# A graph network with a mixture of experts: where VectorE forms the next group's logits, and where the split rows' messages are kept

## The reference, cut to what matters

```python
z = (x @ W).reshape(N, heads, dim)
el = sum(z * attn_l); er = sum(z * attn_r)          # one number per node and head
e = leaky_relu(el[src] + er[dst], 0.2)
alpha = softmax of e over the edges of each dst
out = segment_sum(alpha * z[src], dst) + z + bias
```

## Time and profile before

| | |
|---|---|
| median of 3 runs | 3047.59 us (3047.36 to 3049.39) |
| profiled execution | 3049.01 us |
| its span, first to last instruction | 3047.3 us |
| mean granted TensorE clock | 0.966 |
| TensorE busy in the span | 88% |
| VectorE, ScalarE, GpSimd busy | 67%, 41%, 49% |
| edge sweeps (ends rounded) | 250 to 893, 1097 to 1741, 1940 to 2582 us |

### The profile page before, as it was taken

One profiled execution on the slowest core, in us unless ns is written; L12 is line 12 of the kernel. 1 busy time (PEld: TensorE's weight loads), 2 busy tenths in 40 slices (PEclk: granted clock), 3 DMA queues, 4 the chain that ended last, 5 costly groups with the idle time before them and its releaser, 6 DMA issues.

```text
span 3047.3 us, 57262 instructions
## 1 busy us (share of the span) xinstructions
PE 2681.5 (88%) x14059; PEld 1839.2 (60%) x14060; DVE 2055.3 (67%) x3890; ACT 1244.9 (41%) x2607; POOL 1495.0 (49%) x1528
## 2 busy tenths in 40 slices
PE   3997999998989979999899899788899888659998
PEld 2884555555558855555555588555555555447776
DVE  6776888888887768888878877455555555663332
ACT  1224555555554445555555544222323223521111
POOL 1005666666632156666666411466666664114443
PEclk9998999999999979999999999799999999979999
DMA  6448988989968889999989678888888998967776
GB/s 211 167 146 269 304 306 303 304 306 302 305 203 213 212 247 305 303 307 304 306 299 306 231 199 221 237 295 297 294 300 298 294 297 270 406 211 146 145 146 119
DMA packets 218702, 787.26 MB, mean 258 GB/s; under 512 B 44050, under 2 KB 75938, under 8 KB 217983
## 3 DMA queue, kind: packets, MB, share of 16 engines
q0 software_dynamic: 127632, 604.14, 63.8%
q1 hardware_dynamic: 73230, 133.39, 14.3%
q10 hardware_dynamic: 17760, 48.79, 4.0%
HBM read 665.13 MB, written 133.50 MB: 262 GB/s over the span
## 4 chain that ended last, share of the span: by engine, by line
PE 53%; DVE 22%; issue 13%; ACT 3%; another core or an unknown queue 3%; DMA 2%; SPq 2%; POOL 1%; DVEq 1%; ACTq 1%; POOLq 0%
PE PS L1026 29%; DVE arena L1466 6%; PE PS L957 5%; PE PS L1153 5%; PE PS L1142 4%; PE PS L959 3%; DVE parts L1483 3%; PE PS L1001 2%; DVE W L1466 2%; DMA arena<-table,src_k 2%; SPq L479 1%; DVE arena L1341 1%; DVE arena L1330 1%; DVE arena L1331 1%
## 5 line engine op out<-in xcount | busy, mean ns | idle before, releaser
L652 POOL DMA_INDIRECT arena<-table,src_k x945 | 946.9, 1002 | 488.6 <-issue 225.2
L1026 PE MATMUL PS<-arena,S 128*128 128x384 f32 (+1 forms) x1848 | 694.7, 509 | 58.6 <-issue 49.5
L1466 DVE TENSOR_TENSOR arena<-arena,PS 128x768 f32<-128x768 f32 x630 | 575.0, 945 | 0.9 <-issue 0.5
L1026 PEld LDWEIGHTS PS<-arena,S 128*128 128x128 f32 x1848 | 333.0, 192 | 275.3 <-issue 142.3
L1026 PE MATMUL PS<-parts,S 128*128 128x384 f32 (+2 forms) x1332 | 338.6, 374 | 54.2 <-issue 41.3
L652 POOL DMA_INDIRECT W<-table,src_k x300 | 297.8, 993 | 155.4 <-issue 68.9
L1026 PE MATMUL PS<-arena,S_weighted 128*128 128x384 f32 (+1 forms) x840 | 318.7, 515 | 35.3 <-issue 32.9
L1001 PEld LDWEIGHTS PS<-erp,ST_b 128*128 128x128 bf16 x3735 | 194.8, 97 | 240.6 <-issue 173.1
L598 POOL DMA_DIRECT2D table<-arena x75 | 41.7, 555 | 560.1 <-DVEq L1353 384.2
L809 ACT ACTIVATE apart<-iota_row,dst_k 128x128 f32<-128x128 f32 x830 | 261.5, 389 | 58.4 <-issue 34.4
L1026 PEld LDWEIGHTS PS<-parts,S 128*128 128x128 f32 x1332 | 223.5, 192 | 99.8 <-issue 90.2
(11 more groups left out here) (286 smaller groups left out, 4275.1 us busy)
## 6 DMA issues: line engine op xcount, KB each, us to landing
local_b<-local SPq DMA_DIRECT2D x249, 160.0 KB
mixed<-sums ACTq DMA_DIRECT2D x75, 384.0 KB
arena<-mixed SPq DMA_DIRECT2D x75, 384.0 KB, 4.3
table<-arena POOLq DMA_DIRECT2D x50, 396.0 KB, 3.6
arena<-table SPq DMA_DIRECT2D x50, 384.0 KB, 4.8
arena<-table,src_k POOLq DMA_INDIRECT x945
table<-arena POOLq DMA_DIRECT2D x25, 384.5 KB, 4.8
out<-last_bias POOLq DMA_DIRECT2D x25, 384.0 KB, 6.3
```

Of the source, the lines that this page charges most:

```text
L652: nc.gpsimd.indirect_dma_start(edge_row(l, k % U)[:, 0:table_width(l)], None, table[l][:, :], bass.IndirectOffsetOnAxis(src_k[:, k:k + 1]. ...
L1026: o = nc.tensor.matmul(flat[:, bass.ds(odd * 1024 + 512 * c, n)], onehot, row[:, c * HALF:c * HALF + n], start=False, stop=True, skip_grou ...
L1466: nc.vector.tensor_tensor(z, z, a, ALU.mult).then_inc(s_msg, 1)
```

## The change

- `ER_LEAD` becomes 2, and two groups share a bank: `group_bank(jj)` is bank 4 + jj % 2. TensorE makes the destination terms of group g + 2 in one batch of 15 matmuls, ahead of visit 4 of group g and behind a wait for that group's fifth message.
- Banks 6 and 7 hold one row, `exact_row`. With 12 heads VectorE writes a split row's message there instead of in place, and copies its 12 weights beside it (a new small instruction); ScalarE and the subtraction read it there. The message waits until the split row before it has its rest. Where rows j - 2 and j are both split (10 and 12), the rest of j - 2 stands ahead of message j.
- With one head ScalarE makes the scaled row once more, in fp32, in `exact_row` (a new instruction and a new wait for the rest before), and the rest is a plain subtraction from it.
- VectorE does all steps of the next group's logits, and then `turned`, behind the fifth message of the group.
- With one head the column numbers are copied into two banks rather than four.

```diff
-ER_LEAD = 3
+ER_LEAD = 2
...
         def group_bank(jj):
-            return PS[:, 4 + jj, :]
+            return PS[:, 4 + jj % 2, :]
...
+        def exact_row(n):
+
+            return flat_banks(6)[:, 0:n]
...
                         if H > 1:
-                            nc.scalar.activation(parts[:, n, 0, 0:D + H], row[:, 0:D + H], ACT.Copy).then_inc(s_leading, 1)
+                            nc.scalar.activation(parts[:, n, 0, 0:D + H], exact_row(D + H), ACT.Copy).then_inc(s_leading, 1)
                         else:
                             weight = row[:, D:D + 1]
+                            act.wait_ge(s_rest, len(SPLIT[l]) * i + (n + split_before(l)))
+                            nc.scalar.activation(exact_row(D), row[:, 0:D], ACT.Copy, scale=weight)
...
                         for j in range(G):
+                            if j == G - 1 and ahead:
+                                pe.wait_ge(s_msg, g * G + (V * l + G))
+                                for n in range(G):
+                                    er_of_edges(g + ER_LEAD, (jj + ER_LEAD) % NBUF, n, later[n])
                             add_up(g, i, jj, j, now[j])
                             if j == 0 and ahead:
                                 later = blocks_of(g + ER_LEAD)
-                            if j in (1, 3) and ahead:
-                                for n in ((0, 1), (2, 3, 4))[j // 2]:
-                                    er_of_edges(g + ER_LEAD, (jj + ER_LEAD) % NBUF, n, later[n])
...
-                        nc.vector.tensor_tensor(z, z, a, ALU.mult).then_inc(s_msg, 1)
+                        if at in SPLIT[l]:
+                            held = SPLIT[l].index(at) + split_before(l)
+                            if not isinstance(i, int) or i or held:
+                                dve.wait_ge(s_rest, len(SPLIT[l]) * i + held)
+                            nc.vector.tensor_tensor(exact_row(D).rearrange("p (h d) -> p h d", h=H), z, a, ALU.mult)
+                            nc.vector.tensor_copy(exact_row(D + H)[:, D:D + H], weights_of(l, jj)[:, j, :]).then_inc(s_msg, 1)
+                        else:
+                            nc.vector.tensor_tensor(z, z, a, ALU.mult).then_inc(s_msg, 1)
...
-                        nc.vector.tensor_tensor(low[:, 0:D + H], row[:, 0:D + H], f32(high[:, 0:D + H]), ALU.subtract).then_inc(s_rest, 1)
+                        nc.vector.tensor_tensor(low[:, 0:D + H], exact_row(D + H), f32(high[:, 0:D + H]), ALU.subtract).then_inc(s_rest, 1)
...
-                        nc.vector.scalar_tensor_tensor(out=low[:, 0:D], in0=row[:, 0:D], scalar=weight,
-                                                       in1=f32(high[:, 0:D]), op0=ALU.mult, op1=ALU.subtract).then_inc(s_rest, 1)
+                        nc.vector.tensor_tensor(low[:, 0:D], exact_row(D), f32(high[:, 0:D]), ALU.subtract).then_inc(s_rest, 1)
...
+                        late = H > 1 and j >= 2 and jj * G + j - 2 in SPLIT[l]
+                        if late and jj * G + j in SPLIT[l]:
+                            rest(g, i, jj, j - 2)
                         message(g, i, jj, j)
-                        if H > 1 and j >= 2 and jj * G + j - 2 in SPLIT[l]:
+                        if late and jj * G + j not in SPLIT[l]:
                             rest(g, i, jj, j - 2)
-                        if j == 1 and turn_next:
-                            turned(g + NBUF, i + 1, jj)
-                        if steps and 1 <= j <= min(3, len(steps)):
-                            steps[j - 1]()
-                        if j == 3 and steps and H == 1:
-                            steps[3]()
+                    if steps:
+                        for step in steps:
+                            step()
+                    if turn_next:
+                        turned(g + NBUF, i + 1, jj)
```

More of the change, by code:

```diff
@@ L1514, in edge_sweep @@
                 if H == 1:
-                    for jj in range(NBUF):
+                    for jj in range(2):
                         o = nc.vector.tensor_copy(columns(jj), iota_row[:, :])
```

## The result

The changed kernel takes 3171.6 us (3163.7 to 3172.6, 4 runs), the kernel before 3048.5: a ratio of 1.0393, 95% interval 1.0379 to 1.0407. The forecast was 3072, the range ended at 3122. The direction was right, and the loss is 123 us where 25 were forecast.

What follows compares the result with a forecast made beforehand. It took the beat of about 7.6 us per group, set by reported finished visits, as the bound. Profiled 3049.0 us +25 (third groups) +0 (one head) -1 = 3073, stated as 3072 for the runs' median; range 3008 to 3122.

Steps and rivals of the forecast that it cites:

- The chain and the group without closings: VectorE, 12 heads: logits to first message 1.06 us; a group 6.44 us with one split row, 8.99 with two.
- The stall in the third group: Visits 10 to 14, 12 heads: row 10's subtraction waits for ScalarE's copy, message 12 follows; 1.4 to 1.7, taken as 1.5 us.
- The closing: ScalarE closes a block in 25 of 83 groups: 1.85 us, all onto the third group's stall, some 0.7 in others.
- The mean against the beat: VectorE's mean group with 12 heads, near 7.4 us, stays just under the beat; only single groups lose time.
- the beat: About 7.6 us per group of five visits in all three edge sweeps, set by when TensorE's visits are reported finished.
- The sweep with one head: Groups 7.1 us with two split rows, 4.1 with one, mean about 6 with closings; VectorE stood idle there: net 0.
- The upper bound of 84 us: Loss from third groups' overruns with 12 heads if VectorE's lead covers nothing: 42 x (1.45 + 0.30 x 1.85).
- Operands in PSUM at zero: VectorE's and ScalarE's whole-row instructions on PSUM cost as from SBUF; ends -21 to +42 us, taken as zero.
- Rival 1: The beat holds in all sweeps whatever VectorE does: no change, 3047 us; chance 0.20.
- Rival 2: Logits no longer hold up ready messages, TensorE gets visits earlier, GpSimd idles less: 33 to 66 us faster, 3015; chance 0.28.
- Rival 3: GpSimd's gathers shorten from a mean of 1002 ns to 0.95 us: 62 us if passed on whole, 2985; chance 0.05.
- The shared banks, priced at nothing: TensorE's batch of 15 matmuls: waiting for message 5 adds nothing; 0.7 us if TensorE caught up, within the 84 us.

Runs made afterwards that it cites:

- late_alone: Kernel before, with only VectorE's next-group logits and turned one-hots moved behind the fifth message; 2964.3 us, ratio 1.0552 to the kernel before, on a faster chip.
- late_2: Kernel before, with only VectorE's next-group logits and turned one-hots moved behind the fifth message, on a slower chip; 3060.1 us, ratio 1.0034 to the kernel before.
- psum12_only: Changed kernel with the one-head sweep's split rows as before (no second scaled row, rest by multiply and subtract); 3150.3 us, ratio 1.0337 to the kernel before, slower chip.
- late_oh_2: Kernel before with late logits, ScalarE's one-hots ahead of the weights and its closing behind them; 3053.2 us, ratio 1.0010 to the kernel before, slower chip.
- act_order: Changed kernel with ScalarE's list in the order one-hots, closing, weights; 2942.1 us, ratio 1.0470 to the kernel before, on a faster chip.
- split4: Changed kernel with row 10 multiplied whole in the 12-head layers, so no group has two split rows; 2930.0 us, ratio 1.0413 to the kernel before, faster chip.

## Why the prediction was right in direction and wrong in size

**The chain and the group without closings: right.** 6.44 and 8.99 us were forecast, 6.33 to 6.8 and 9.37 measured. The stall in the third group came to 1.85 us for 1.5, since ScalarE's leading part starts 3.2 to 3.3 us behind the weights and not 2.4 to 2.8: the register load between the two was not in the sum. The chain from logits to message was 1.04 us (511.96 to 513.00) for 1.06, and the turned one-hots lay in its gap.

**The closing: the step that failed.** "1.85 in all (an estimate)", "in the third group all of it goes onto the stall, in the others some 0.7". A closing put ScalarE's leading part 3.0 to 4.0 us later (means by place). Of that 2.4 to 2.8 us reached VectorE in the groups with one split row and 3.6 to 4.0 in the third. Two things were wrong. The price left out ScalarE's queue: on the faster chips, where nothing is stretched, a closing costs 2.8 to 3.0 us, 2.0 for the instructions and the small gaps between them and 0.8 for the second register load and the branches (1.37 us before the closing instead of 0.61); on the slower chips up to 1.5 us of stretched register steps come on top. And the part passed on was set too low: late_alone shows 2.25 us of stall behind each closing even with none of the PSUM changes. Before, ScalarE could be late by this much, for the next logits and weights were already under way; the 0.7 kept some of the old cover that late logits had taken away. In sum that is (2.6 - 0.7) x 17/71 + (3.8 - 1.85) x 4/71, some 0.6 us a group in the mean (71 groups counted, 21 with a closing, 4 of these third groups). The groups without a closing, 7.2 in the mean for the 7.08 forecast, give the last 0.1 from 7.4 to 8.09.

**The mean against the beat: failed with it.** At 7.4 us "nothing is lost against the mean"; at 8.09 every group loses 0.5 us: over the 79 groups up to the last gather 40 us a sweep, and the last visit ends 27.8 us after the start of the last gather instead of 20.1, another 8. Twice that, 96 us, is nearly the 98 that the two sweeps show. The upper bound of 84 us priced only the third groups and was no bound. Nor did the range take it in, as the prediction says: 3048 + 84 is 3132, and the range ends at 3122. In late_2, where the mean stays near the beat, the loss is 10 us.

**The sweep with one head: failed.** Net 0 was forecast from a mean of 6 us. ScalarE's second row takes 0.91 us as supposed, and groups with two split rows take 7.5 and 8.1 us without a closing where 7.1 was forecast, those with one 5.3 and 5.9 where 4.1 was. With a closing they take 11.2 and 11.9, and 9.0 and 9.6: a closing adds over 3.5 us to each, so the mean is 7.8 and not 6. The waits at the rests come to 208 us in 500, and the sweep got 24 to 27 us longer. psum12_only takes 23 of these back, so the new form of the split rows makes them; how much of it is the second row and how much the wait for the shared one, no run tells apart.

**Operands in PSUM at zero: right.** Groups by form of the changed kernel:

```profile
L656 POOL DMA_INDIRECT arena<-table,src_k x945 | 902.0, 954 | 618.4 <-PE PS L1032 387.6 <-issue 201.0 <-remote 24.6
...
L1497 DVE TENSOR_TENSOR parts<-PS,parts 128x780 fp32r<-128x780 f32 x208 | 200.5, 964 | 213.4 <-ACT parts L765 171.5 <-issue 41.8
...
L765 ACT ACTIVATE parts<-PS 128x780 fp32r<-128x780 f32 x208 | 167.8, 807 | 101.1 <-DVE PS L1478 79.8 <-issue 18.6 <-PE PS L1032 2.2
...
L1477 DVE TENSOR_TENSOR PS<-arena,PS 128x768 f32<-128x768 f32 x168 | 161.1, 959 | 8.6 <-ACT arena L807 4.7 <-issue 2.5
...
L769 ACT ACTIVATE PS<-arena 128x768 f32<-128x768 f32 x105 | 95.0, 905 | 102.7 <-issue 65.3 <-DVE parts L1501 20.0 <-PE PS L1032 12.4
...
L1478 DVE COPY PS<-PS 128x12 f32<-128x12 f32 x208 | 35.6, 171 | 0.0
```

A whole-row write to PSUM takes 959 ns against 946 in place, the rest 964 against 965, the leading part 807 against 850, the small copy 171.

**Rivals.** Rival 1 holds nearly in late_2 (0.34%) and in late_oh_2 (0.10%), where the beat hides the change, and fell for the whole change. Rival 2: the waits of the logits, 70 us in 500, fell to 5 in the changed kernel, but stalls at the rests took their place. The better test is late_oh_2: its logits wait 3 us in 500, the messages 51 us for weights or issue and the rests 19, and no time is won on a slower chip. Rival 3 is half right: the mean gather from `table` into `arena` fell from 1002 to 954 ns. The Trainium skill has it so ("SBUF — State Buffer", Who interferes with whom): a VectorE instruction with two SBUF inputs contends with what GpSimd reads from SBUF, one with at most one does not. The runs agree, sweep by sweep: where the subtractions read the row in PSUM the mean gather is 947 to 965 ns, and where they have two SBUF inputs 978 to 1065. psum12_only turns this back in the last sweep alone, and there alone the mean rises, from 951 to 1023. No time came of it: GpSimd's idle time before these gathers rose from 488.6 to 618.4 us. The shared banks, priced at nothing, cost nothing with late logits on a faster chip.

## What to carry to other kernels

When a step is moved so that two engines hand work back and forth once per group, add up the whole round, with every wait and rare branch in the other engine's list between the two hand-overs; slack that covered them before is gone. Price rare branches with the register loads and branch steps of the engine's queue, which no list of busy instructions shows, and look into the queue before a wait is put down to another engine. Then compare the resulting mean, not only its outliers, with the pace that holds the loop. One shared buffer between two engines costs most where two of its users stand close together, and reordering the other engine's list may give back most of it (78 of 124 us here).

## What the runs showed of the hardware

- Chips of one kind differ: the kernel before takes 3048 to 3051 us in the median on three and 2810 to 2814 on two others, though gathers (0.95 us undisturbed) and messages (0.95) take the same time. On the slower ones no variant had a sweep under 7.5 us a group, on the faster 6.25 was seen (the last sweep of act_order).
- One thing that differs in the traces is the queues of TensorE and ScalarE. In all twelve traces from slower chips 135 to 219 register or branch steps of TensorE's queue and 43 to 106 of ScalarE's take over 0.5 us, most of them 0.70; in the eight from faster chips none does, the longest takes 0.24. The same line of split4, on a faster chip, beside that of the changed kernel above:

```profile
L815 ACTq FUSED_REGOPS  x760: 37/46/57, 298.3 to 1620.8; - x190
```

- TensorE's signals of finished visits differ as well. From 300 to 800 us of the four traces of the kernel before, 98 to 118 of some 320 come within 0.1 us of the one before (517.26, 517.32, 517.38 us, after a pause from 512.09), and GpSimd's first gather of a run follows such a signal (517.52). In the eight traces from faster chips none does. What stretches the steps and bunches the signals, and whether the first makes the second, is open, and with it what makes the beat.
- How much a lost microsecond shows depends on the beat: late logits alone cost 0.34% on a slower chip and 5.5% on the faster. The ratio of 1.039 is that of the slower chips.
